# Who fills the query rows with zeros: ScalarE in eight pieces in the place of two GpSimd memsets

## The chip, the cores and the metric

The kernel runs on one core of a Trainium2 chip. Its five engines work on their own instruction streams and meet only at semaphores: TensorE (PE, with its weight loads PEld), VectorE (DVE), ScalarE (ACT), GpSimd (POOL) and SyncE (SP), which here issues the DMAs. The metric is the device time of one execution in microseconds; lower is better. Three executions of the kernel before took 801.71, 802.96 and 804.95 us, so the median is 802.96 us.

## The reference

The program computes three residual steps on x, which is 2 x 1024 tokens of width 256:

```python
x = x + 0.5 * ffn(layernorm(x))      # silu(x Wg) * (x Wu), 2 of each 4 kept by size, then Wd; inner width 1024
x = x + attention(layernorm(x))      # 32 query heads, 8 key/value heads, head size 8, rotary, causal
x = x + 0.5 * ffn(layernorm(x))      # the same weights
```

In attention, q, k and v come from one projection of the normed x, q and k are turned by the rotary tables, and each group of four query heads shares one key/value head:

```python
q = x @ Wq + bq ; k = x @ Wk + bk ; v = x @ Wv + bv
q = q*cos + rotate_half(q)*sin ; k = k*cos + rotate_half(k)*sin
attn = softmax(causal(q k^T / sqrt(8))) ; out = (attn v) @ Wo + bo
```

Two batches times eight key/value heads make 16 groups, each with 4 query heads over 1024 tokens.

## The kernel before

**Phases.** The program is four phases, one after the other on each engine: the first feed-forward network, the projection to q, k and v, attention over 16 groups, the second feed-forward network. Matmuls that must keep float32 precision are done as three products of high and low parts (hi x hi, hi x lo, lo x hi), so every operand is split: a copy rounded to the multiplier's format makes the high part, and a subtraction makes the low part.

**The projection phase** is the one that the change touches. It goes over four chunks c = 0 to 3 of 512 tokens, and in each chunk over three units u = 0, 1, 2 (two halves of q, and k). A unit passes through the engines like this:

- PE multiplies (L218, twelve matmuls of 512 columns for a unit), signals `qk_done`. Between unit 1 and unit 2 of a chunk it transposes the normed x of the next chunk (`normed.transpose`, L188), for which it waits for DVE's `v_ready` (L733) and `xn_ready`. After unit 0 it does the matmuls for v (L751).
- DVE adds the bias and multiplies by cos and by sin (L815, L817), and signals `by_ready`.
- POOL adds the two products: `qkv_turned` (L859).
- ACT copies that to the high part in `qkv_parts` (L790, `high`).
- POOL subtracts for the low part (L864, `low`).
- SP stores both parts to DRAM (L895), as rows that attention will load.

POOL takes the units strictly in order, `add_turned` then `low` then the next `add_turned`, so it waits for ACT in the middle of each unit. ACT, too, has one order, written out in `chunk`: high part of unit 0; the first half of the next chunk's transposed x (L195); high part of unit 1; the second half of the transposed x (L195 again, after all units of the chunk are multiplied); high part of unit 2. The second half of the transposed x is thus queued behind the high part of unit 1. DVE does the normalisation of the chunk after the next transposes (`normalise`, L181, four instructions of 128x256 from SBUF to SBUF), then unit 0, the values v (L823), unit 1, the statistics, the low parts of the transposed x (L199), unit 2.

**The rows of the groups.** `GroupRows` holds two sets of tiles, e = 0 and 1: `q[e]`, 128 partitions by 4 heads by 1024 tokens, and `k[e]`, 128 by 1024. Only some partitions of them are loaded; the others must hold zeros in q and -1 in k. So before the first load into set e, the whole tile is filled, once in the program: `fill_q` (L961) and `fill_k` (L964), both POOL memsets, and SP waits for them in front of `load_m` (L902, L908). They stand in the list `fills`, of which POOL does item c after chunk c (L878): q0 after chunk 0; k0 and the causal mask (L1635, L1637, in `before_groups`) after chunk 1; q1 and k1 after chunk 2.

**Into attention.** The first four products of attention (`first_scores`) stand ahead of the last unit of chunk 3 on PE. After them comes a lead-in: PE multiplies q by k for the row maxima (L1371), DVE takes the maxima (L1471, L1474), POOL splits them into shifts (L1586, L1588), PE transposes the shift (L1379), ACT copies it (L1530), SP writes it into the q rows (L1647), and only then do the scores that ACT exponentiates start (L1406, L1524), followed by the products with v (L1422).

## Time and profile before

| what | value |
|---|---|
| median of three executions | 802.96 us (801.71 to 804.95) |
| span of the profiled execution, first to last instruction | 799.2 us |
| the profiled execution's own time | not recorded apart from its span; the median is 3.8 us above that span |
| PE busy / DVE busy | 752.0 us (94%) / 712.8 us (89%) |
| ACT busy / POOL busy | 487.9 us (61%) / 263.3 us (33%) |
| mean granted PE clock | 0.974 of full speed |
| projection phase | from about 172 to 221 us of the span |
| the two q fills on POOL | 3.52 us each |
| the two k fills on POOL | 0.95 us each |

How to read it: times are from the start of the span. Busy shares over the whole span mix phases with different limits; the change lies in the 50 us of the projection phase, and what it is worth is read there. A row of a timeline gives start, duration, engine, line, operation, and in brackets how long the engine had been idle before it and which instruction released it. Back-to-back instructions of DVE, ACT and POOL are shown with a small overlap, since the next one starts before the last has fully ended.

### The profile page before, as it was taken

The page shows a single profiled execution, that of the slowest core. Times are in us where ns is not written, and L with a number is a line of the kernel's source. Part 1 is how long each engine was busy: PE and PEld are TensorE (multiplying, and loading weights), DVE is VectorE, ACT ScalarE, POOL GpSimd, SP SyncE. Part 2 cuts the span into 40 slices and gives each one's busy share as a digit, 9 for nine tenths or more (in the row PEclk, how much of TensorE's full clock was granted, in tenths as well). Part 3 has the DMA queues.
Part 4 walks back from the last instruction along what each step waited for, and adds up shares of the span by engine and source line. Part 5 has one row for each costly group of instructions (what it writes and reads, how often), then busy time and mean ns, then how long its engine had stood idle before and what let it go on. Part 6 is the DMA issues. An engine that isn't in the chain of part 4 may idle for free.

```text
span 799.2 us, 15470 instructions
## 1 busy us (share of the span) xinstructions
PE 752.0 (94%) x5168; PEld 503.9 (63%) x5168; DVE 712.8 (89%) x1857; ACT 487.9 (61%) x949; POOL 263.3 (33%) x359
## 2 busy tenths in 40 slices
PE   4899999988999999999999999999999999999996
PEld 3677887886855444554444544444544577888886
DVE  4989999988598999999999999999996459989997
ACT  6454443321124888888888888888888634344451
POOL 1143535027742222333222332255335211533330
PEclk9999999999965999999999999999999999999998
DMA  8100000015753033431133321633223000000001
GB/s 305 44 12 1 1 1 1 1 52 185 218 179 68 11 70 76 89 73 43 40 76 75 75 62 47 159 78 76 62 55 75 16 8 1 1 27 1 27 1 52
DMA packets 23551, 48.83 MB, mean 61 GB/s; under 512 B 3784, under 2 KB 10568, under 8 KB 22960
## 3 DMA queue, kind: packets, MB, share of 16 engines
q1 hardware_dynamic: 23408, 47.78, 22.8%
q8 instruction: 41, 0.67, 0.4%
q14 instruction: 38, 0.31, 0.1%
q10 hardware_dynamic: 64, 0.07, 0.0%
HBM read 19.83 MB, written 14.35 MB: 43 GB/s over the span
## 4 chain that ended last, share of the span: by engine, by line
PE 64%; DVE 19%; POOL 6%; issue 5%; ACT 4%; DMA 1%; PEldq 0%; PEld 0%; SPq 0%; DVEq 0%; ACTq 0%; POOLq 0%
PE att_o_ps L1422 18%; PE att_s_ps L1406 15%; PE att_m_ps L1371 11%; PE ffn_gate L218 6%; PE ffn_up L218 5%; PE ffn_y_ps L351 5%; DVE ffn_hs L524 3%; DVE ffn_h L566 3%; POOL qkv_turned L859 2%; POOL qkv_parts L864 2%; PE att_m_ps L1379 1%; DVE att_scratch L1471 1%; DVE ffn_rank L510 1%; DVE ffn_pair_max L498 1%; PE out_y_ps L1162 1%
## 5 line engine op out<-in xcount | busy, mean ns | idle before, releaser
L1524 ACT ACTIVATE att_probs<-att_s_ps 128x512 f32<-128x512 f32 x630 | 305.7, 555 | 54.7 <-PE att_s_ps L1406 52.9
L1471 DVE CUSTOM_DVE_ANT_0 att_scratch<-att_m_ps,att_causal 128x512 bf16<-128x512 f32 (+3 forms) x512 | 221.1, 486 | 7.7 <-PE att_m_ps L1371 6.1
L1371 PE MATMUL att_m_ps<-k,q 64*128 64x512 f32 (+3 forms) x768 | 222.8, 399 | 2.4 <-DVE att_maxima L1471 1.9
L1406 PE MATMUL att_s_ps<-q,k 64*128 64x512 f32 (+2 forms) x756 | 209.9, 384 | 2.7 <-ACT att_probs L1524 1.0
L1406 PEld LDWEIGHTS att_s_ps<-q,k 64*128 64x128 f32 x756 | 118.2, 188 | 97.0 <-ACT att_probs L1524 91.5
L1474 DVE TENSOR_REDUCE att_maxima<-att_m_ps 128x1 f32<-128x512 f32 x256 | 161.9, 684 | 7.2 <-PE att_m_ps L1371 7.1
L1422 PE MATMUL att_o_ps<-att_probs,att_vs 128*32 128x512 f32 (+3 forms) x1536 | 158.5, 500 | 3.2 <-POOL att_probs L1563 1.6
L1563 POOL TENSOR_SCALAR_AFFINE_SELECT att_probs<-att_probs 128x512 f32<-128x512 f32 x128 | 80.0, 637 | 245.3 <-ACT att_probs L1524 245.3
L1371 PEld LDWEIGHTS att_m_ps<-k,q 64*128 64x128 f32 x768 | 128.1, 193 | 42.0 <-DVE att_maxima L1471 24.4
L630 POOL TENSOR_TENSOR ffn_hs_lo<-ffn_hs,ffn_hs_hi 128x512 fp32r<-128x512 f32 x48 | 76.7, 1622 | 106.5 <-ACT ffn_hs_hi L427 106.5
L454 ACT ACTIVATE ffn_a<-ffn_h 128x512 f32<-128x512 f32 x64 | 40.5, 633 | 106.3 <-DVE ffn_h L566 106.3
L351 PE MATMUL ffn_y_ps<-wd_hi,ffn_hs_hi 128*128 128x256 f32 x256 | 73.8, 288 | 6.3 <-DVE x L554 2.7
L351 PE MATMUL ffn_y_ps<-wd_lo,ffn_hs_hi 128*128 128x256 f32 x256 | 72.9, 285 | 0.0
L351 PE MATMUL ffn_y_ps<-wd_hi,ffn_hs_lo 128*128 128x256 f32 x256 | 72.8, 284 | 0.0
L1422 PEld LDWEIGHTS att_o_ps<-att_probs,att_vs 128*32 128x32 f32 x1536 | 34.1, 108 | 54.9 <-issue 42.0
L566 DVE TENSOR_TENSOR ffn_h<-ffn_up,ffn_silu 128x512 f32<-128x512 f32 x64 | 43.6, 682 | 22.8 <-ACT ffn_silu L449 21.8
L218 PE MATMUL ffn_gate<-ffn_xt_hi,wg_hi 128*128 128x512 f32 x128 | 52.2, 408 | 4.7 <-DVE ffn_h L566 2.7
L351 PEld LDWEIGHTS ffn_y_ps<-wd_hi,ffn_hs_hi 128*128 128x128 f32 x256 | 49.4, 193 | 9.4 <-DVE x L554 2.9
L218 PE MATMUL ffn_gate<-ffn_xt_lo,wg_hi 128*128 128x512 f32 x128 | 50.8, 397 | 0.9 <-DVE ffn_xt_lo L199 0.9
L427 ACT ACTIVATE ffn_hs_hi<-ffn_hs 128x512 fp32r<-128x512 f32 x56 | 35.0, 633 | 27.1 <-DVE ffn_hs L524 27.1
L218 PE MATMUL ffn_gate<-ffn_xt_hi,wg_lo 128*128 128x512 f32 x128 | 50.9, 398 | 0.0
L351 PEld LDWEIGHTS ffn_y_ps<-wd_lo,ffn_hs_hi 128*128 128x128 f32 x256 | 49.5, 193 | 1.6
(117 smaller groups left out, 1176.5 us busy)
## 6 DMA issues: line engine op xcount, KB each, us to landing
q_rows<-qkv_parts SPq DMA_DIRECT2D x16, 512.0 KB, 4.0
q<-q_rows SPq DMA_DIRECT2D x16, 512.0 KB, 4.7
q<-q SPq DMA_DIRECT2D x16, 512.0 KB, 4.3
q<-att_shift_t SPq DMA_DIRECT2D x132, 4.0 KB
k_rows<-qkv_parts SPq DMA_DIRECT2D x8, 256.0 KB, 3.0
k<-k_rows SPq DMA_DIRECT2D x16, 128.0 KB, 4.9
k<-k SPq DMA_DIRECT2D x16, 128.0 KB, 4.6
out_num<-att_sums SPq DMA_DIRECT2D x128, 16.0 KB
```

The source lines that it names most:

```text
L218: last = pe.matmul(bank, w[w_part], xt[:, k, :], start=(k == 0 and n == 0), stop=(k == self.KT - 1 and n == 2))
L351: last = pe.matmul(y_ps[:, t, :], hp[:, blk, j, rows], wp[:, blk, j, :], start=(blk == 0 and j == 0 and m == 0 and t % 2 == 0), stop=(blk ...
L454: act.activation(a[:, blk, j, :], h[:, blk, j, :], ACT.Abs).then_inc(abs_ready, 1)
L566: dve.tensor_tensor(h[:, blk, j, :], gu[j % 2][1][:], silu[:, j % 2, :], ALU.mult).then_inc(h_ready, 1)
L630: pool.tensor_tensor(hs_lo[:, blk, j, :], hs[:, j, :], hs_hi[:, blk, j, :].bitcast(F32), ALU.subtract).then_inc(lo_ready, 1)
L1371: pe.matmul(m_ps[unit_bank(n)][:, COLUMNS[m]], q[g % 2][m_lane, h, t * P:(t + 1) * P], k[g % 2][m_lane, kc * N:kc * N + cols], start=True, ...
L1406: last = pe.matmul(s_all[S_BANK[n]][:, at:at + w], k[g % 2][lane, kb * P:(kb + 1) * P], q[g % 2][lane, h, qc * N + q0:qc * N + q0 + w], st ...
L1422: last = pe.matmul(o_ps[32 * h:32 * (h + 1), q0:q0 + w], vs[g % 2][:, kb, :], probs[u % len(probs)][:, h, at:at + w], start=(u in CHUNK_FI ...
L1471: dve.tensor_tensor_reduce(out=scratch[bank][:, at], in0=m_ps[bank][:, at], in1=causal[:, N - n:], scale=1.0, scalar=LOWEST, op0=ALU.add, ...
L1474: dve.tensor_reduce(top_of, m_ps[bank][:, at], mybir.AxisListType.X, ALU.max).then_inc(m_taken, 1)
L1524: act.activation(probs[u % len(probs)][:, h, SPAN[u]], s_all[S_BANK[n]][:, SPAN[u]], ACT.Exp, scale=SCALE).then_inc(exp_done, 1)
L1563: pool.affine_select(out=blk, in_=blk, compare_op=ALU.is_ge, fill=0.0, base=0, pattern=[[0, QPK], [1, P]], channel_multiplier=-1).then_inc ...
```

## The change

The q fills move from POOL to ACT. Each 128x4096 memset becomes four ACT copies of 128x1024, one for each head, whose input is a one-column zero tile read again and again. The zero tile is set by one small POOL memset at the start of the phase. Set 0 is filled behind the high part of unit 2 in chunk 0, set 1 behind the high part of unit 2 in chunk 1. On POOL, the k0 fill moves up into the place of the q0 fill (behind chunk 0), the causal mask stays behind chunk 1, and only the k1 fill is left behind chunk 2. SP waits for ACT's fills on a new semaphore beside the old one.

```diff
--- before.py
+++ after.py
@@ -782,6 +782,8 @@
         dve.wait_ge(w_hi_ready, 1)
         dve.tensor_tensor(w_lo[:], w_raw, w_hi[:].bitcast(F32), ALU.subtract).then_inc(w_lo_ready, 1)
 
+    FILLS = {(e, UNITS - 1): [(e, h) for h in range(group_rows.QPK)] for e in range(2)}
+
     def scalar(act):
         def high(c, u):
             n = c * UNITS + u
@@ -796,11 +798,14 @@
                     act.wait_ge(normed.xt_used, FIRST + c + 1)
                     normed.high_parts(act, FIRST + c + 1, 0)
                 high(c, u)
+                for e, h in FILLS.get((c, u), ()):
+                    group_rows.fill_q(act, e, h)
                 if turn:
                     act.wait_ge(qk_done, (c + 1) * UNITS)
                     for k in range(1, KT):
                         normed.high_parts(act, FIRST + c + 1, k)
 
+        act.wait_ge(group_rows.zero_ready, 1)
         for c in range(0, CHUNKS - 1):
             chunk(c)
         chunk(CHUNKS - 1, last=True)
@@ -871,6 +876,7 @@
                 if u == 1 and c + 2 < CHUNKS:
                     normed.inverse_deviation(pool, FIRST + c + 2)
 
+        pool.memset(group_rows.zero[:], 0.0).then_inc(group_rows.zero_ready, 1)
         normed.inverse_deviation(pool, FIRST + 1)
         for c in range(CHUNKS):
             chunk(c)
@@ -899,13 +905,15 @@
         for c in range(FIRST_BATCH):
             store(c)
         group_rows.wait_stored(sp, FIRST_BATCH)
-        sp.wait_ge(group_rows.filled, 2)
+        sp.wait_ge(group_rows.filled, 1)
+        sp.wait_ge(group_rows.q_filled, group_rows.QPK)
         group_rows.load_m(sp, 0)
         for c in range(FIRST_BATCH, CHUNKS):
             store(c)
             if c == FIRST_BATCH:
                 group_rows.copy_s(sp, 0)
-                sp.wait_ge(group_rows.filled, 4)
+                sp.wait_ge(group_rows.filled, 2)
+                sp.wait_ge(group_rows.q_filled, 2 * group_rows.QPK)
                 group_rows.load_m(sp, 1)
 
     def banks_free(pe, bank):
@@ -943,7 +951,10 @@
             self.at[e] = region.at
             self.q.append(region.take(f"q{e}", [P, self.QPK, T], F32R))
             self.k.append(region.take(f"k{e}", [P, T], F32R))
+        self.zero = region.take("zero", [P, 1], F32)
+        self.zero_ready = ctx.enter_context(nc.semaphore("zero_ready"))
         self.filled = ctx.enter_context(nc.semaphore("rows_filled"))
+        self.q_filled = ctx.enter_context(nc.semaphore("rows_q_filled"))
         self.s_loaded = [ctx.enter_context(nc.semaphore(f"s_loaded{e}")) for e in range(2)]
 
         self.m_loaded = [ctx.enter_context(nc.semaphore(f"m_loaded{e}")) for e in range(2)]
@@ -957,8 +968,8 @@
             for sem in sems:
                 sp.wait_ge(sem, 16 * chunks)
 
-    def fill_q(self, pool, e):
-        pool.memset(self.q[e][:].rearrange("p h t -> p (h t)").bitcast(F32), 0.0).then_inc(self.filled, 1)
+    def fill_q(self, act, e, h):
+        act.activation(self.q[e][:, h, :], self.zero[:].to_broadcast([P, self.T]), ACT.Copy).then_inc(self.q_filled, 1)
 
     def fill_k(self, pool, e):
         pool.memset(self.k[e][:].bitcast(F32), -1.0).then_inc(self.filled, 1)
@@ -1823,9 +1834,7 @@
         output = Output(nc, ctx, late, hole, x, w_o.rearrange("(k p) n -> p k n", p=P), den_rows, inverse_rows, KVH, C // HD // KVH, HD, T, N, out_ps)
         attention, before_groups, first_scores, first_maxima, hooks = attention_programs(
             nc, ctx, group_rows, v, att_region, s_ps, m_ps, m_spare, o_ps, output, normed2, ident_bf, x, bo, T, HD, earlier)
-        between["fills"] += [lambda pool: group_rows.fill_q(pool, 0),
-                    lambda pool: (group_rows.fill_k(pool, 0), before_groups(pool)),
-                    lambda pool: (group_rows.fill_q(pool, 1), group_rows.fill_k(pool, 1))]
+        between["fills"] += [lambda pool: group_rows.fill_k(pool, 0), before_groups, lambda pool: group_rows.fill_k(pool, 1)]
         between["first_scores"], between["first_maxima"] = first_scores, first_maxima
         assert att_region.at <= late_at
         homes2 = Homes(s_hole, {**dict.fromkeys(("ffn2_silu", "ffn2_rank", "ffn2_both_low", "ffn2_tilt"), late_hole), "ffn2_hs": m_hole})
```

On POOL, the rows around the end of chunk 0 and the end of chunk 1, before (line 859 adds the two rotary products, line 864 subtracts for the low part, k_52 and q_51 are the tiles of set 0):

```order
L859 TENSOR_TENSOR qkv_turned<-qkv_by_cos,qkv_by_sin 128x512
L864 TENSOR_TENSOR qkv_parts<-qkv_turned,qkv_parts 128x512
L961 MEMSET q_51 128x4096
L859 TENSOR_TENSOR qkv_turned<-qkv_by_cos,qkv_by_sin 128x512
...
L864 TENSOR_TENSOR qkv_parts<-qkv_turned,qkv_parts 128x512
L964 MEMSET k_52 128x1024
L1635 MEMSET att_causal 128x512
L1637 AFFINE_SELECT att_causal<-att_causal 128x128
L859 TENSOR_TENSOR qkv_turned<-qkv_by_cos,qkv_by_sin 128x512
```

The same stretch of POOL in the changed kernel, where lines 859 and 864 have become 864 and 869:

```order
L864 TENSOR_TENSOR qkv_turned<-qkv_by_cos,qkv_by_sin 128x512
L869 TENSOR_TENSOR qkv_parts<-qkv_turned,qkv_parts 128x512
L975 MEMSET k_52 128x1024
L864 TENSOR_TENSOR qkv_turned<-qkv_by_cos,qkv_by_sin 128x512
...
L869 TENSOR_TENSOR qkv_parts<-qkv_turned,qkv_parts 128x512
L1646 MEMSET att_causal 128x512
L1648 AFFINE_SELECT att_causal<-att_causal 128x128
L864 TENSOR_TENSOR qkv_turned<-qkv_by_cos,qkv_by_sin 128x512
```

Behind chunk 0 a memset of 4096 columns has given way to one of 1024, and behind chunk 1 the k fill is gone from ahead of the mask.

On ACT, from the last unit of chunk 0 to the first unit of chunk 2, before (line 790 is the high part of a unit, line 195 a half of the transposed x):

```order
L195 ACTIVATE ffn_xt_hi<-ffn_xt_ps 128x512
L790 ACTIVATE qkv_parts<-qkv_turned 128x512 x2
L195 ACTIVATE ffn_xt_hi<-ffn_xt_ps 128x512
L790 ACTIVATE qkv_parts<-qkv_turned 128x512
L195 ACTIVATE ffn_xt_hi<-ffn_xt_ps 128x512
L790 ACTIVATE qkv_parts<-qkv_turned 128x512 x2
```

The same stretch of ACT in the changed kernel, with the high part now at line 792:

```order
L195 ACTIVATE ffn_xt_hi<-ffn_xt_ps 128x512
L792 ACTIVATE qkv_parts<-qkv_turned 128x512
L972 ACTIVATE q_51<-zero 128x1024 x4
L792 ACTIVATE qkv_parts<-qkv_turned 128x512
L195 ACTIVATE ffn_xt_hi<-ffn_xt_ps 128x512
L792 ACTIVATE qkv_parts<-qkv_turned 128x512
L195 ACTIVATE ffn_xt_hi<-ffn_xt_ps 128x512
L792 ACTIVATE qkv_parts<-qkv_turned 128x512
L972 ACTIVATE q_53<-zero 128x1024 x4
L792 ACTIVATE qkv_parts<-qkv_turned 128x512
```

Each pair of high parts that ran over the end of a chunk now has four fill copies between its two members. PE's and DVE's own order is unchanged.

## Rows read from the trace of the kernel before

**Rows 1.** The page: engines, and the chain that ended last by engine.
```profile
PE 752.0 (94%) x5168; PEld 503.9 (63%) x5168; DVE 712.8 (89%) x1857; ACT 487.9 (61%) x949; POOL 263.3 (33%) x359
...
PE 64%; DVE 19%; POOL 6%; issue 5%; ACT 4%; DMA 1%; PEldq 0%; PEld 0%; SPq 0%; DVEq 0%; ACTq 0%; POOLq 0%
```
**Rows 2.** Timeline of PE: start us, us, instruction, [idle before, releaser].
```profile
174.60 1.09 PE L188 MATMUL ffn_xt_ps<-ident,ffn_xn 128*128 128x128 f32 x8 [1.88 <-DVE v L823]
...
190.85 1.94 PE L188 MATMUL ffn_xt_ps<-ident,ffn_xn 128*128 128x128 f32 x8 [3.65 <-DVE qkv_by_sin L817]
...
204.38 1.03 PE L188 MATMUL ffn_xt_ps<-ident,ffn_xn 128*128 128x128 f32 x8
...
209.98 0.50 PE L218 MATMUL qkv_plain<-ffn_xt_hi,qkv_w_hi 128*128 128x512 f32 x1 [0.38 <-ACT ffn_xt_hi L195]
...
231.12 0.59 PE L1379 MATMUL att_m_ps<-ident_bf,att_shift 128*8 128x128 bf16 x4 [0.26 <-POOL att_shift L1588]
```
**Rows 3.** Timeline of DVE around the normalisation behind chunk 0.
```profile
182.26 6.84 DVE L181 TENSOR_SCALAR ffn_xn<-x,ffn_mean_var,ffn_rstd 128x256 f32<-128x256 f32 x4 [0.20 <-POOL ffn_rstd L175]
189.02 0.73 DVE L815 SCALAR_TENSOR_TENSOR qkv_by_cos<-qkv_plain,qkv_biases,qkv_cos 128x512 f32<-128x512 f32 x1
...
190.34 0.41 DVE L823 TENSOR_TENSOR v<-ffn_xt_ps,qkv_bv 128x256 f32<-128x256 f32 x1
```
**Rows 4.** Line 181 alone, 186 to 190 us and whole span: min/median/max ns.
```profile
L181 DVE TENSOR_SCALAR ffn_xn<-x,ffn_mean_var,ffn_rstd x1: 4922/4922/4922, 184.2 to 184.2; 128x256 f32<-128x256 f32 x1
...
L181 DVE TENSOR_SCALAR ffn_xn<-x,ffn_mean_var,ffn_rstd x48: 400/406/4922, 10.4 to 733.9; 128x256 f32<-128x256 f32 x48
```
**Rows 5.** Timeline of POOL, projection phase.
```profile
184.21 1.29 POOL L864 TENSOR_TENSOR qkv_parts<-qkv_turned,qkv_parts 128x512 fp32r<-128x512 f32 x1 [0.74 <-ACT qkv_parts L790]
185.44 3.52 POOL L961 MEMSET q<- 128x4096 f32 x1
190.50 1.27 POOL L859 TENSOR_TENSOR qkv_turned<-qkv_by_cos,qkv_by_sin 128x512 f32<-128x512 f32 x1 [1.54 <-DVE qkv_by_sin L817]
...
199.02 1.37 POOL L859 TENSOR_TENSOR qkv_turned<-qkv_by_cos,qkv_by_sin 128x512 f32<-128x512 f32 x1 [0.31 <-DVE qkv_by_sin L817]
...
202.36 0.95 POOL L964 MEMSET k<- 128x1024 f32 x1
203.25 0.53 POOL L1635 MEMSET att_causal<- 128x512 f32 x1
...
204.20 1.29 POOL L859 TENSOR_TENSOR qkv_turned<-qkv_by_cos,qkv_by_sin 128x512 f32<-128x512 f32 x1
...
215.29 3.52 POOL L961 MEMSET q<- 128x4096 f32 x1
```
**Rows 6.** Timeline of ACT, chunks 1 and 2.
```profile
191.80 0.63 ACT L790 ACTIVATE qkv_parts<-qkv_turned 128x512 fp32r<-128x512 f32 x1 [7.67 <-POOL qkv_turned L859]
...
208.81 0.63 ACT L790 ACTIVATE qkv_parts<-qkv_turned 128x512 fp32r<-128x512 f32 x1 [1.37 <-POOL qkv_turned L859]
209.35 0.58 ACT L195 ACTIVATE ffn_xt_hi<-ffn_xt_ps 128x512 fp32r<-128x512 f32 x1
```
**Rows 7.** ACT groups by form, 238 to 247 us: count, busy us, mean ns.
```profile
L1524 ACT ACTIVATE att_probs<-att_s_ps 128x512 f32<-128x512 f32 x8 | 4.3, 597 | 0.4 <-PE att_s_ps L1406 0.2
L1524 ACT ACTIVATE att_probs<-att_s_ps 128x256 f32<-128x256 f32 x4 | 1.4, 383 | 1.0 <-PE att_s_ps L1406 1.0
```
**Rows 8.** Windows: PE, PEld, DVE, ACT, POOL busy, then granted clock.
```profile
190.80:194.20 3.40, 3.35 (x12) 3.09 (x13) 2.90 (x10) 0.63 (x1) 2.66 (x3) 0.51 0.26 98
225.00:249.00 24.00, 23.39 (x72) 14.23 (x72) 23.59 (x84) 8.84 (x16) 8.66 (x18) 0.50 0.31 98
249.00:259.00 10.00, 10.00 (x45) 4.70 (x49) 7.19 (x24) 3.50 (x7) 0.61 (x3) 0.50 0.62 136
259.00:279.00 20.00, 19.55 (x170) 9.49 (x162) 18.99 (x70) 16.86 (x37) 4.59 (x10) 1.00 0.03 6
```
**Rows 9.** Timeline of SP's queue: the first load of set 0.
```profile
205.60 0.34 SPq L975 DMA_DIRECT2D q<-q_rows  x1
```

## The prediction, made before the changed kernel was run

> **What bounds the kernel now.** Read the page first [rows 1]: PE is busy 94% of the span and holds 64% of the chain that ended last, while the engine that loses work here, POOL, is busy 33%. Taken over the span, 7 us of POOL time would be worth nothing. So look at the one place where the chain runs through POOL, the projection phase, and ask PE's timeline where PE stood still [rows 2]. The reader is to see one large hole: before the transposes behind unit 1 of chunk 1 PE is idle 3.65 us, up to 190.85. It waits for DVE. DVE's timeline [rows 3] shows why DVE is late: four normalisations took 6.84 us together, and the values v, on which the transposes also wait, came only at 190.34. The rows of line 181 alone [rows 4] show that one of the four, started at 184.2, took 4.92 us, where the median of all 48 is 0.41 us. POOL's timeline [rows 5] has the cause: the low part ran from 184.21 to 185.50 and the q0 memset from 185.44 to 188.96, and the slow instruction ended at 189.10, 0.14 us behind the memset. The same POOL waited 1.54 us afterwards, for the DVE that it had held up.
>
> The second thing to see is what carries a delay on. At 209.98 PE waits again, 0.38 us, for the second half of the transposed x on ACT [rows 2]. That copy stands at 209.35 right behind the high part of unit 1, which had waited for POOL's `qkv_turned` [rows 6]. So from chunk 2 on the tight chain is POOL to ACT to PE, and PE's own earliness counts only as far as that chain follows.
>
> Attention then takes the shift over whole. From 259 us PE is busy 19.55 of 20 us at full clock, and in the lead-in from 225 to 249 us DVE is busy 23.59 of 24 [rows 8]. Work that is full on one engine starts earlier and ends earlier, and nothing in it is tied to a time.
>
> **The change, part by part.**
>
> *q0 memset away, k0 memset in its place.* What stands behind the low part of chunk 0 falls from 3.52 to 0.95 us [rows 5]. I take it that the blocked normalisation waits through this memset as it did through the longer one, and so ends at 186.5, not 189.1: 2.57 us earlier. Bounds: none of it, if something else had held that instruction (0), and all of the memset (3.5) if the k fill is not waited for. I choose 2.57, since the end of the slow instruction sits 0.14 us behind the end of the memset, and a k fill is the same instruction with fewer columns.
>
> The Trainium skill speaks against this reading of the blocking. "SBUF — State Buffer", section "Who interferes with whom", says that DVE in a two-port mode and GpSimd exclude each other for the whole of one instruction, and that issue order decides who blocks. By that the waiting DVE instruction would have got in at 185.5, between the low part and the memset; the trace shows it waiting through both. Page and row agree that the two block each other, but not on when the loser gets its turn. I go by the row; the other reading is a rival below, 0.7 us better.
>
> *The clock.* In the stretch 190.8 to 194.2 the granted clock is 0.51, the lower level of 1.2 GHz, behind the idle 3.65 us, and the eight transposes take 1.94 us against 1.03 in the next chunk [rows 2, 8]. At half speed 3.35 us busy hold 1.7 us of full-speed work, so the low stretch costs 1.7. With the hole cut to 3.65 - 2.57 = 1.1 us I expect no fall: the idle 1.88 us before 174.60 brought none, as the transposes after it took 1.09 us [rows 2]. PE is then 2.6 + 1.7 = 4.3 us earlier. Bounds 0 and 1.7.
>
> *What the POOL chain lets through.* POOL starts chunk 1 2.57 us earlier, at 187.9. Walking its three units with the durations of the rows (1.29 for each sum and difference, 0.74 for the trip to ACT and back), the sum of unit 2 comes at 195.7 instead of 199.02 [rows 5]: 3.3 us, since PE's halves of x are no longer late as well. Then the k0 fill is gone from between chunks 1 and 2, 0.9 us with its overlap, and the first sum of chunk 2 starts at 200.0 instead of 204.20: 4.2 us.
>
> *The new ACT copies.* A copy of 128x1024 is not in the trace. The exponentials of 512 and 256 columns take 597 and 383 ns, so 256 columns cost 214 and 1024 columns about 1.03 us, four of them 4.1, or 3.9 when they overlap [rows 7]. Bounds: 0.60 each, as for 512 columns, and 1.19, two of 512, so 2.4 to 4.8 us for four. Behind chunk 0 they run from 184.15 to about 188.1, and the next high part is wanted at 189.2; before, ACT sat idle 7.67 us here [rows 6], so they are free even at the upper bound. What stands behind them is only that high part. Behind chunk 1 there is less room: the high part of unit 2 would end near 197.8, the copies near 201.8, and POOL's first sum of chunk 2 is ready at 201.3. The high part waits 0.5 us, and POOL, DVE and PE behind it. Bounds 0 and 1.3. So 4.2 - 0.5 = 3.7 us arrive where PE waits at 209.98, less than PE's own 4.3.
>
> *Chunk 2's fills.* The q1 memset, 3.52 us at 215.29 [rows 5], is not on PE's path: the sums behind it feed stores and nothing that PE reads. It does hold back the first shift of attention: PE waited 0.26 us for it at 231.12 [rows 2]. That wait goes, and what is late next is DVE's maxima, 3.7 us earlier like the rest. I count 0.2.
>
> *Waits and queues.* SP now waits for the q fill (done by 188.2) and the k fill (186.4) before its load of set 0, which went out at 205.60 behind the stores of chunk 1 [rows 9]. These stores end last by 13 us or more, so the new wait is free; its cover is chunk 1's own stores. For set 1 the fills end near 201.8 on ACT and 212 on POOL, long before the lead-in needs that set. The zero tile's memset runs where POOL waits for DVE, and the first ACT wait on it follows that by microseconds: 0.
>
> Sum against the profiled execution: 3.7 + 0.2 = 3.9 us off a span of 799.2, giving 795.3. The median stands 3.8 above that span, so the time is 802.96 - 3.9 = 799.1 us.
>
> **The rivals.**
>
> *Only the stall goes (2.6 us).* The clock falls at 187 all the same, or the four copies cost their upper bound behind chunk 1, so that 3.7 shrinks to 2.9 or less. For it: in the lead-in the clock is low from 225 us on although PE counts as busy 23.39 of 24 us [rows 8], so a long hole is not the only thing that brings it down. Against it: the 1.88 us before 174.60. Time 802.96 - 2.6 = 800.4.
>
> *The waiting instruction gets in at once.* If DVE's fourth normalisation runs between low part and k fill, it ends 0.7 us sooner, and the chain is 0.7 us further ahead: 4.6 us, 798.3. The 4.92 us of [rows 4] speak against it. (It is what the rule of the Trainium skill in "SBUF — State Buffer" would give.)
>
> *The low clock in the lead-in ends sooner.* From 225 to 259 the clock is at its low level [rows 8]. To 249 that costs next to nothing, as DVE is full. From 249 to 259 DVE is busy only 7.19 of 10 us, against 18.99 of 20 afterwards, so these 10 us cost 2.3. A lead-in shifted by 4 us might meet the rise earlier: up to 2.3 more, 796.8.
>
> *The stall was hidden anyway.* Another wait takes the place of the hole, for instance ACT's halves of x held by POOL in chunk 1 as in chunk 2. The walk above leaves them 3.3 us or more ahead, which speaks against it. Time 803.0.
>
> *Slower: the low clock lasts into attention's steady part.* It rose at 259, when products with v had begun to fill PE. There PE has no slack (19.55 of 20 us), and each further low microsecond costs between 0.24, as from 249 to 259, and 0.5, half the speed. If the shifted lead-in misses the rise by 15 us, it costs 7.5: 802.96 - 3.9 + 7.5 = 806.6. It decides from 3.9 / 0.5 = 8 us on. Against it: the instruction order on PE is the same, and the rise comes with that order.
>
> **How the numbers follow.** Within 0.5% (4.0 us) a measurement of this kernel can't tell from no change, and the forecast of 3.9 lies on that edge. Chances: forecast 0.46, only the stall 0.20, in at once 0.05, low clock sooner 0.13, hidden 0.08, slower 0.08. The forecast splits about evenly over the edge, so faster is 0.23 + 0.05 + 0.13 + a little from a base that shifts = 0.44, same 0.23 + 0.20 + 0.06 = 0.49, slower 0.07. The range: the forecast's own is 797.8 to 800.4; it must reach 796.8 less a little for the noise of 1.6 us half-width, and up to the hidden case: 795.8 to 802.8. Outside are the slower case, half of the hidden one, and the tail below.
>
> **What would show it right or wrong.** In the profile after: line 181 in chunk 0 with a slowest instruction near 2.35 us (4.92 less 2.57); PE's wait before the second set of transposes near 1.1 us, and their eight matmuls in 1.0 to 1.1 us at clock 1.00; POOL's first sum of chunk 2 at 200 to 200.5 us; four ACT copies in 3.9 to 4.1 us; ACT's high part of unit 0 in chunk 2 right behind the fourth copy, without a wait for POOL; the first load of set 0 some 3 us earlier, released by the stores. The forecast is wrong if the slow normalisation stays at 4.9 us, if PE's hole moves instead of shrinking, or if the windows at full clock begin later than 259 us.

## The result, and the profile after

The changed kernel took 797.57 us in the median (797.05 to 800.30, 6 runs) against 802.44 us of the kernel before (6 runs, the three from above among them). One of the six runs before, 830.46 us, was slow as a whole and is left out of the ratio, so the ratio is not the quotient of these two medians (0.9939). It is 0.9951, 95% interval [0.9934, 0.9967]: 0.49% faster, or 3.9 us of the 802.96 that the forecast started from, with 2.6 to 5.3 us inside the interval. The forecast was 799.1, that is 0.9952. The profiled span fell from 799.2 to 796.1 us.

The profile's page shows what moved: POOL lost 6.7 us of busy time, ACT gained 7.3, and POOL's share of the chain halved from the 6% of [rows 1].

```profile
PE 752.0 (94%) x5168; PEld 504.4 (63%) x5168; DVE 709.1 (89%) x1857; ACT 495.2 (62%) x957; POOL 256.6 (32%) x358
...
PE 66%; DVE 19%; issue 5%; ACT 5%; POOL 3%; DMA 1%; PEldq 0%; PEld 0%; SPq 0%; DVEq 0%; ACTq 0%; POOLq 0%
```

PE's timeline after, for [rows 2] (L1390 is the old L1379):

```profile
174.52 1.40 PE L188 MATMUL ffn_xt_ps<-ident,ffn_xn 128*128 128x128 f32 x8 [1.93 <-DVE v L828]
...
188.19 1.04 PE L188 MATMUL ffn_xt_ps<-ident,ffn_xn 128*128 128x128 f32 x8
...
200.77 1.06 PE L188 MATMUL ffn_xt_ps<-ident,ffn_xn 128*128 128x128 f32 x8 [0.47 <-DVE qkv_by_sin L822]
...
227.21 0.59 PE L1390 MATMUL att_m_ps<-ident_bf,att_shift 128*8 128x128 bf16 x4
```

The hole of 3.65 us is gone altogether, not cut to 1.1, and so is the wait for `ffn_xt_hi` at 209.98. A wait of 0.47 us stands before the third transposes. I measure every kernel below from the first row to the last of these, from chunk 0's transposes to the first transposes of attention's shift; call it the **stretch**. It was 231.12 - 174.60 = 56.52 us before and is 52.69 after: 3.83 less.

DVE's normalisations after, behind chunks 0 and 1, for [rows 3], and line 181 over the whole span, for [rows 4]:

```profile
182.67 2.33 DVE L181 TENSOR_SCALAR ffn_xn<-x,ffn_mean_var,ffn_rstd 128x256 f32<-128x256 f32 x4
...
195.18 3.85 DVE L181 TENSOR_SCALAR ffn_xn<-x,ffn_mean_var,ffn_rstd 128x256 f32<-128x256 f32 x4 [0.19 <-POOL ffn_rstd L175]
```

```profile
L181 DVE TENSOR_SCALAR ffn_xn<-x,ffn_mean_var,ffn_rstd x48: 396/408/1933, 10.2 to 730.8; 128x256 f32<-128x256 f32 x48
```

Behind chunk 0 four normalisations took 2.33 us together: the slowest took 1.36 us, through one POOL instruction (the sum at 182.83), and none waited through the k fill. The slowest of all 48, 1.93 us, is now behind chunk 1. It started at 197.1 and so waited through the low part and the mask's memset, to 199.03.

POOL's timeline after, for [rows 5]:

```profile
184.94 1.29 POOL L869 TENSOR_TENSOR qkv_parts<-qkv_turned,qkv_parts 128x512 fp32r<-128x512 f32 x1 [0.74 <-ACT qkv_parts L792]
186.16 0.95 POOL L975 MEMSET k<- 128x1024 f32 x1
187.08 1.29 POOL L864 TENSOR_TENSOR qkv_turned<-qkv_by_cos,qkv_by_sin 128x512 f32<-128x512 f32 x1
189.24 1.30 POOL L869 TENSOR_TENSOR qkv_parts<-qkv_turned,qkv_parts 128x512 fp32r<-128x512 f32 x1 [0.87 <-ACT qkv_parts L792]
...
195.11 1.26 POOL L864 TENSOR_TENSOR qkv_turned<-qkv_by_cos,qkv_by_sin 128x512 f32<-128x512 f32 x1
197.12 1.29 POOL L869 TENSOR_TENSOR qkv_parts<-qkv_turned,qkv_parts 128x512 fp32r<-128x512 f32 x1 [0.74 <-ACT qkv_parts L792]
198.35 0.53 POOL L1646 MEMSET att_causal<- 128x512 f32 x1
...
200.42 1.28 POOL L864 TENSOR_TENSOR qkv_turned<-qkv_by_cos,qkv_by_sin 128x512 f32<-128x512 f32 x1 [1.09 <-DVE qkv_by_sin L822]
```

The 1.09 us in the last row is the new wait: POOL, freed of the k fill here, waits for the DVE that it has blocked. ACT's timeline after, for [rows 6]:

```profile
184.76 3.88 ACT L972 ACTIVATE q<-zero 128x1024 fp32r<-128x1024 f32 x4
188.55 0.61 ACT L792 ACTIVATE qkv_parts<-qkv_turned 128x512 fp32r<-128x512 f32 x1
...
196.95 3.88 ACT L972 ACTIVATE q<-zero 128x1024 fp32r<-128x1024 f32 x4
201.73 0.63 ACT L792 ACTIVATE qkv_parts<-qkv_turned 128x512 fp32r<-128x512 f32 x1 [0.91 <-POOL qkv_turned L864]
```

Four copies take 3.88 us. Behind chunk 0 the high part follows them at once, and POOL waits 0.87 us for it instead of the usual 0.74: there the copies fill ACT's gap and 0.13 us more. Behind chunk 1 ACT is done 0.91 us before it is wanted, so these copies are hidden. The windows after, for [rows 8]:

```profile
225.00:249.00 24.00, 23.70 (x79) 14.14 (x78) 22.13 (x81) 8.21 (x15) 4.12 (x10) 0.50 0.16 44
249.00:257.00 8.00, 8.00 (x46) 3.92 (x46) 5.78 (x16) 4.20 (x8) 0.00 (x0) 0.50 0.60 138
257.00:277.00 20.00, 19.54 (x162) 9.69 (x160) 19.06 (x69) 16.97 (x36) 4.57 (x10) 1.00 0.04 10
```

The clock is back at its upper level, 2.4 GHz, from 257 us on, 2 us earlier than before, although the work came 3.8 us earlier.

### The profile page after: what moved, and what is told of

Its sections match the earlier page's. It is cut to its first block, busy times and chain, and to the rows that moved or that the text cites. A ratio compares the mean times of both kernels' runs of the same rounds, so it can differ in the third digit from the quotient of the medians.

```text
span 796.1 us, 15479 instructions
## 1 busy us (share of the span) xinstructions
PE 752.0 (94%) x5168; PEld 504.4 (63%) x5168; DVE 709.1 (89%) x1857; ACT 495.2 (62%) x957; POOL 256.6 (32%) x358
## 4 chain that ended last, share of the span: by engine, by line
PE 66%; DVE 19%; issue 5%; ACT 5%; POOL 3%; DMA 1%; PEldq 0%; PEld 0%; SPq 0%; DVEq 0%; ACTq 0%; POOLq 0%
PE att_o_ps L1433 18%; PE att_s_ps L1417 15%; PE att_m_ps L1382 12%; PE ffn_gate L218 5%; PE ffn_up L218 5%; PE ffn_y_ps L351 5%; DVE ffn_h L566 3%; DVE ffn_hs L524 3%; DVE att_scratch L1482 2%; PE att_m_ps L1390 1%; DVE ffn_rank L510 1%; DVE ffn_pair_max L498 1%; DVE ffn_pair_min L499 1%; PE out_y_ps L1173 1%; DVE ffn_first_wins L501 1%
## 5 line engine op out<-in xcount | busy, mean ns | idle before, releaser
L566 DVE TENSOR_TENSOR ffn_h<-ffn_up,ffn_silu 128x512 f32<-128x512 f32 x64 | 43.6, 681 | 22.9 <-ACT ffn_silu L449 21.9
L218 PE MATMUL ffn_up<-ffn_xt_hi,wu_hi 128*128 128x512 f32 x128 | 50.4, 394 | 0.0
```

The lines of the kernel that those rows point to most:

```text
L218: last = pe.matmul(bank, w[w_part], xt[:, k, :], start=(k == 0 and n == 0), stop=(k == self.KT - 1 and n == 2))
L566: dve.tensor_tensor(h[:, blk, j, :], gu[j % 2][1][:], silu[:, j % 2, :], ALU.mult).then_inc(h_ready, 1)
```

## The experiments

Two theories compete; each expectation spells out its own. **P**: the chain POOL to ACT to PE of the projection pays for every microsecond that POOL spends on fills behind chunks 0 and 1, and the 3.65 us hole was only the face of it that showed. **L**: the price is the lock, the normalisation held by POOL, with PE's hole and the fallen clock. All ratios are to the kernel before, for e1 to e12 run on the same chip as the experiment, with 95% intervals; each stretch is from one trace; the stretch was 56.52 us before.

| run | ratio | stretch, us |
|---|---|---|
| the change | 0.9951 [0.9934, 0.9967] | 52.69 |
| the change again (e9) | 0.9952 [0.9935, 0.9969] | 52.64 |
| q0 alone on ACT (e1) | 0.9968 [0.9953, 0.9983] | 53.43 |
| the same again (e10) | 0.9956 [0.9942, 0.9969] | 53.05 |
| q1 alone on ACT (e2) | 0.9998 [0.9985, 1.0010] | 55.34 |
| before, memset in four (e3) | 1.0011 [1.0000, 1.0023] | 56.23 |
| before, q0 and k0 fills swapped (e4) | 1.0020 [1.0005, 1.0035] | 57.02 |
| all eight copies behind chunk 0 (e5) | 0.9993 [0.9980, 1.0006] | 55.66 |
| before, ACT normalises (e6) | 1.0011 [0.9995, 1.0027] | 59.67 |
| the change, ACT normalises (e7) | 0.9962 [0.9948, 0.9975] | 53.82 |
| the change, k0 fill behind chunk 1 (e8) | 0.9959 [0.9943, 0.9975] | 53.54 |
| half of the q0 fill on ACT (e11) | 0.9971 [0.9959, 0.9982] | 54.54 |
| the change, mask late (e12) | 0.9952 [0.9933, 0.9971] | 52.91 |

**One part alone: e1 and e2.**

```diff
-    FILLS = {(e, UNITS - 1): [(e, h) for h in range(group_rows.QPK)] for e in range(2)}
+    FILLS = {(e, UNITS - 1): [(e, h) for h in range(group_rows.QPK)] for e in (0,)}   # e1; (1,) in e2
```

The other set keeps its memset on POOL, at its old place (in e2 the k0 fill, too).

> Only the q0 fill moves to ACT (and the k0 fill into its place behind chunk 0); the q1 fill stays a 3.52 us POOL memset behind chunk 2. Theory: the whole gain comes from what POOL no longer does behind chunk 0, and the fill behind chunk 2 is off PE's path but for the first shift (0.2 us). So ratio about 0.9953 to the kernel before (797.57/802.44 is 0.994 to 0.9967 by the runs), and POOL's first sum of chunk 3 near 216 instead of 212.41 us with no later PE. Rival: the q1 fill is worth as much as the q0 fill, since both are 3.52 us of POOL: then the ratio is about 0.998.

> Only the q1 fill moves to ACT, behind chunk 1; the q0 memset stays behind chunk 0 and the k0 fill behind chunk 1, as before. Theory: PE's hole of 3.65 us and the low clock after it stay, so the ratio is 1.000 (0.9990 to 1.0005); ACT's four copies behind chunk 1 are hidden. Rival: each fill is worth half, ratio 0.998; second rival, the copies are in the way, ratio 1.001.

The q0 fill carries the gain: 0.9968 for it alone (e10 measures it again, at 0.9956), and no difference that can be measured for q1 alone. The telling thing is PE's timeline of e2, where the q0 memset is still on POOL:

```profile
186.69 1.06 PE L188 MATMUL ffn_xt_ps<-ident,ffn_xn 128*128 128x128 f32 x8 [0.19 <-issue]
190.95 0.47 PE L218 MATMUL qkv_plain<-ffn_xt_hi,qkv_w_hi 128*128 128x512 f32 x1 [0.39 <-ACT ffn_xt_hi L195]
194.12 0.50 PE L218 MATMUL qkv_plain<-ffn_xt_hi,qkv_w_hi 128*128 128x512 f32 x1 [1.54 <-ACT ffn_xt_hi L195]
202.78 1.06 PE L188 MATMUL ffn_xt_ps<-ident,ffn_xn 128*128 128x128 f32 x8 [1.52 <-DVE qkv_by_sin L822]
```

Here the hole before the second transposes is missing, the clock did not fall, and yet the time is that of before (0.9998; the interval allows 1.2 us less). The normalisations behind chunk 0 took 3.38 us: the last one got in ahead of the memset. PE instead stood three times, 3.45 us in all, for ACT's halves of x behind POOL's late sums and for DVE behind chunk 1. That speaks for P, but it is no kernel without a lock: behind chunk 1 the normalisations were blocked for 4.75 us in all. Nor is the long lock free. Up to here e2 and before are the same program but for the zero tile's small memset, and POOL's first sum of chunk 1 comes 14.50 us behind the transposes of chunk 0 in e2, against 15.90 before. Of these 1.40 us 1.03 are left at the first sum of chunk 2, behind the second lock.

**Memset in four pieces, and swapped with the k fill: e3 and e4** (both on the kernel before).

```diff
+        for h in range(self.QPK):                                             # e3
+            last = pool.memset(self.q[e][:, h, :].bitcast(F32), 0.0)
-        between["fills"] += [lambda pool: group_rows.fill_q(pool, 0),         # e4
-                    lambda pool: (group_rows.fill_k(pool, 0), before_groups(pool)),
+        between["fills"] += [lambda pool: group_rows.fill_k(pool, 0),
+                    lambda pool: (group_rows.fill_q(pool, 0), before_groups(pool)),
```

> The kernel before with each q memset split in four POOL memsets of 1024 columns (0.95 us each, so 3.6 to 3.8 us for four), nothing on ACT. Theory A, the blocked DVE instruction waits until POOL pauses, however many instructions follow each other: line 181's longest in chunk 0 stays near 4.9 to 5.2 us and the ratio is 1.000. Theory B, it gets in at the end of the one POOL instruction that blocks it: line 181's longest is 1.3 to 1.7 us, the hole of PE is under 1 us, and the ratio is 0.995 to 0.997.

> The kernel before with the fills of set 0 exchanged, all on POOL: k0 behind chunk 0, q0 with the causal mask behind chunk 1. Theory: behind chunk 0 it looks like the changed kernel (no hole of 3.65 us), but POOL's first sum of chunk 2 comes 3.5 us later than in the changed kernel (near 204) and PE meets it at chunk 3: about 3 of the 4.9 us are given back, ratio 0.9975 to 0.999. Rival: only what stands behind chunk 0 matters, ratio 0.9950.

In e3 the four pieces took 3.63 us together, and the normalisations behind chunk 0 did not meet them (2.33 us), as DVE had got ahead of POOL. So it says nothing on borders between the pieces. It speaks for P like e2: behind chunk 0 no long lock and no hole, and the time of before. It too has a lock behind chunk 1, 4.74 us for the four, with PE idle for 1.50 us. In e4 I expected a gain and was wrong. The memset met the normalisations behind chunk 1 in full:

```profile
194.78 7.29 DVE L181 TENSOR_SCALAR ffn_xn<-x,ffn_mean_var,ffn_rstd 128x256 f32<-128x256 f32 x4 [0.18 <-POOL ffn_rstd L175]
```

```profile
203.82 1.69 PE L188 MATMUL ffn_xt_ps<-ident,ffn_xn 128*128 128x128 f32 x8 [4.06 <-DVE qkv_by_sin L817]
```

The loss is not tied to chunk 0. Moved by one chunk, it comes back whole.

**How much ACT hides: e5**, all eight copies behind chunk 0.

```diff
+    FILLS = {(0, UNITS - 1): [(e, h) for e in range(2) for h in range(group_rows.QPK)]}
```

> The changed kernel, but all eight ACT copies stand behind chunk 0 (none behind chunk 1). They take 7.8 us there instead of 3.9, from about 184.8 to 192.5, and the high part of unit 0 of chunk 1 is wanted at about 188.4. Theory: ACT's cover behind chunk 0 ends after some 3.6 us, so about 4 us are lost on the chain from POOL over ACT to PE and the gain is gone: ratio 0.999 to 1.001 to the kernel before. Rival: ACT has room, since it is busy only 62% of the span: ratio 0.995 as in the changed kernel.

```profile
188.15 1.28 POOL L864 TENSOR_TENSOR qkv_turned<-qkv_by_cos,qkv_by_sin 128x512 f32<-128x512 f32 x1 [1.54 <-DVE qkv_by_sin L822]
192.51 1.29 POOL L869 TENSOR_TENSOR qkv_parts<-qkv_turned,qkv_parts 128x512 fp32r<-128x512 f32 x1 [3.08 <-ACT qkv_parts L792]
```

Eight copies took 7.66 us and held the high part that POOL waits for: 3.08 us against the usual 0.74. ACT's gap behind a chunk takes the four copies of the change and no more, and the gain is gone (0.9993).

**The lock taken out: e6 and e7.** ACT makes the normalised x of chunks 2 and 3, from x times 1/deviation and a shifted mean that POOL works out, so that DVE has no normalisation there that POOL could block; e6 is the kernel before with this, e7 the changed one.

```diff
+            act.activation(self.xn[:, t, :], self.x_tile(c, t), ACT.Identity, bias=self.minus_mean[:, t:t + 1],
+                           scale=self.rstd[:, t:t + 1]).then_inc(self.xn_ready, 1)
-        if c + 1 < CHUNKS:
+        if c == 0:
             normed.normalise(dve, FIRST + c + 1)
```

> The kernel before, all fills on POOL, but the normalised x of chunks 2 and 3 is made by ACT (with two small POOL instructions for its bias), so no instruction of DVE in these chunks can be blocked by POOL. Theory L, the loss is DVE standing blocked behind the memset: without the block the gain is there although the memset stays, ratio 0.995 to 0.997. Theory P, the loss is the 3.5 us that the memset keeps POOL from its next sum, whoever is blocked: ratio 0.999 to 1.001, PE waits about 1.5 us for ACT's half of x in chunk 2 as in the run with only q1 moved.

> The changed kernel with the normalised x of chunks 2 and 3 made by ACT in the same way. Theory P: the block behind chunk 1 (3.85 us for four instructions, POOL waiting 1.09 us for DVE and PE 0.47 us) goes, against about 0.5 us of added POOL work in each of two chunks and 1.3 us of added ACT work: ratio 0.994 to 0.9955, at best 0.5 us better than the changed kernel. Theory L: another 1.5 us, ratio 0.993.

POOL and PE in e6:

```profile
186.68 3.52 POOL L981 MEMSET q<- 128x4096 f32 x1
190.16 1.26 POOL L878 TENSOR_TENSOR qkv_turned<-qkv_by_cos,qkv_by_sin 128x512 f32<-128x512 f32 x1
```

```profile
192.72 0.47 PE L233 MATMUL qkv_plain<-ffn_xt_hi,qkv_w_hi 128*128 128x512 f32 x1 [1.99 <-ACT ffn_xt_hi L210]
195.88 0.80 PE L233 MATMUL qkv_plain<-ffn_xt_hi,qkv_w_hi 128*128 128x512 f32 x1 [1.07 <-ACT ffn_xt_hi L210]
```

Without any lock in these chunks the kernel before is not faster (1.0011), and the change on top of it still gains: e7 stands at 0.9962. L had the first at 0.995 to 0.997. The aid has a price of its own, and e7 is slower than the 0.994 to 0.9955 that I gave it: ACT's four normalisations take 2.08 us ahead of a high part, for which POOL then waits 1.5 us. So only the difference of e6 and e7 speaks on the memset, 0.5% in time and 5.85 us in the stretch.

Part of that difference is the clock. Behind the wait of 1.99 us PE's clock fell in e6 and stayed low from 193.6 to 207.1 us, while in e7 it was 1.00 from 193 to 207. One window of PE in e6 (busy, then clock):

```profile
196.00:198.00 2.00, 2.00 (x5) 0.50 0.94 337
```

The clean comparison is the one ahead of that fall. POOL's first sum of chunk 1 comes 15.70 us behind the transposes in e6 and 13.20 in e7: 2.50 less, where the two fills on POOL differ by 3.52 - 0.95 = 2.57, with full clock and with no normalisation on DVE. At the first sum of chunk 2 it is 3.17 less; the rest of the 5.85 arises behind it.

**The k0 fill back behind chunk 1: e8** (on the changed kernel).

```diff
-        between["fills"] += [lambda pool: group_rows.fill_k(pool, 0), before_groups, ...
+        between["fills"] += [lambda pool: None, lambda pool: (group_rows.fill_k(pool, 0), before_groups(pool)), ...
```

> The changed kernel, but the k0 fill stays behind chunk 1 with the mask, as before the change, so nothing stands behind chunk 0 on POOL. Theory P: 0.95 us of POOL has only moved from one chunk to the next, ratio 0.9945 to 0.996, no difference to the changed kernel that can be measured. Rival, from my prediction: the k fill gone from chunk 1 was worth 0.9 us, so this kernel is 0.9 us slower than the changed one, ratio 0.9962.

The stretch is 0.85 us longer, about the 0.95 of the fill; the ratios 0.9959 and 0.9951 can't be told apart. So in the stretch the rival, the term of my prediction, was right, and a fill is not worth the same wherever it stands. Behind chunk 0 taking it away gave nothing, as POOL then waited for ACT's copies:

```profile
189.15 1.29 POOL L869 TENSOR_TENSOR qkv_parts<-qkv_turned,qkv_parts 128x512 fp32r<-128x512 f32 x1 [1.55 <-ACT qkv_parts L792]
```

That is 14.65 us behind the transposes, against 14.72 with the k0 fill there (the change). P holds for what POOL spends beyond ACT's copies.

**The change and e1 again: e9 and e10**, word for word the same programs.

> The changed kernel once more, beside the next three on one chip. Theory P (3.5 us of GpSimd time taken out of the chain of the projection phase): ratio 0.995 to 0.996 again, from the transposes of chunk 0 to attention's first transposes 52.7 us as in the first profile. If the hundredths that decide who gets in between two GpSimd instructions vary from run to run of one program, the normalisation behind chunk 0 may now be the blocked one (one instruction of 2.3 us) and that behind chunk 1 not; by P the 52.7 us stay within 0.4.

> The q0 fill alone on ScalarE, the q1 fill left as a memset, measured against the whole change on one chip. The earlier profiles give the q1 fill 0.7 us (53.4 us against 52.7 from the transposes of chunk 0 to attention's first transposes), so ratio 0.0009 above the whole change. If the q1 fill is worth nothing, both ratios agree within 0.0005.

e9 repeats the change: 0.9952, 52.64 us, and again 2.33 us of normalisation behind chunk 0. e10 did not repeat e1's trace: 4.28 us there in e1, 2.33 here, with a stretch of 53.43 and 53.05. Their stretches are 0.4 us apart, and their ratios 0.0004, which is nothing that can be measured. But that 0.4 is not the q1 fill: 0.32 of it is there at POOL's low part of unit 2 in chunk 0, ahead of every fill. From POOL's first sum of chunk 2 to the end of the stretch it takes 26.79 us in e9 and 26.88 in e10, and so it is in all traces without ACT's normalisation: 26.77 to 26.80 where the q1 fill is on ACT, 26.87 to 27.00 where it is on POOL. The q1 fill is worth 0.1 us there; e4 alone stands apart, with the fills exchanged.

**Half the dose: e11**, two heads on ACT, two in a POOL memset ahead of the k0 fill.

```diff
+        pool.memset(self.q[e][:, 2:4, :].rearrange("p h t -> p (h t)").bitcast(F32), 0.0).then_inc(self.filled, 1)
```

> Of the q0 fill two heads go to ScalarE and two stay on GpSimd, one memset of 128x2048, 1.8 us by half of 3.52, ahead of the k0 fill; everything else as in the changed kernel. Theory P, the price is proportional to GpSimd's time: 1.8 us later than the changed kernel at attention's first transposes, 54.5 us instead of 52.7, ratio 0.9973. Rival, the price comes only from the long lock with its idle TensorE and fallen clock: with a blocked normalisation of at most 4.1 us and no fall of the clock most of the gain stays, 53 us, ratio 0.9955.

```profile
185.79 1.81 POOL L975 MEMSET q<- 128x2048 f32 x1
187.54 0.95 POOL L978 MEMSET k<- 128x1024 f32 x1
188.45 1.30 POOL L864 TENSOR_TENSOR qkv_turned<-qkv_by_cos,qkv_by_sin 128x512 f32<-128x512 f32 x1
```

```profile
194.24 0.50 PE L218 MATMUL qkv_plain<-ffn_xt_hi,qkv_w_hi 128*128 128x512 f32 x1 [1.20 <-ACT ffn_xt_hi L195]
202.00 1.06 PE L188 MATMUL ffn_xt_ps<-ident,ffn_xn 128*128 128x128 f32 x8 [0.60 <-DVE qkv_by_sin L822]
```

1.81 us of POOL cost 1.85 to 1.90 us of stretch against the two traces of the change, and 1.49 against e10, with no normalisation behind chunk 0 that waits through a fill (2.33 us) and no hole there. The 0.3 us that these traces differ by ahead of any fill bound how well that is known. P named 54.5 us and 0.9973; measured are 54.54 and 0.9971. L's 53 us is out. Its 0.9955 lies just outside the interval, which begins at 0.9959; as e1 and e10, one program, differ by 0.0012, the ratio alone would not decide it.

**The mask away from behind chunk 1: e12.**

```diff
+        between["fills"] += [lambda pool: group_rows.fill_k(pool, 0), lambda pool: None, lambda pool: (before_groups(pool), group_rows.fill_k(pool, 1))]
```

> The changed kernel with the causal mask's memset and select (0.53 and 0.30 us) moved from behind chunk 1 to behind chunk 2, ahead of the k1 fill. In the changed kernel they stand between the chunks, the normalisation behind chunk 1 waits through them (1.93 us), and TensorE waits 0.47 us. Theory P: the first sum of chunk 2 comes 0.6 to 1.0 us earlier (199.5 to 199.8 instead of 200.4), and attention's first transposes 0.5 to 1 us earlier if the same two instructions behind chunk 2 feed nothing TensorE waits for; ratio 0.994 to 0.995. If the steps behind chunk 1 are not on the chain any more: no difference from the changed kernel.

No difference from e9 (0.9952 both); the gain I gave it did not come. The normalisations behind chunk 1 did shrink, from 3.85 to 3.39 us, but behind chunk 0 they took 4.28 us in this trace, and POOL stood 1.54 us for DVE at both places. POOL's third sum of chunk 1 came 0.73 us later in the stretch than in e9, its first of chunk 2 only 0.27 us later: the mask's share is the 0.46 us between. No version beat the change.

## Why the prediction was right

The forecast of 3.9 us less came out: 3.83 and 3.88 us of stretch in two traces, ratios 0.9951 and 0.9952. The mechanism held in its core: the fill on POOL held back the chain POOL to ACT to PE. Several terms were wrong in size, and they cancelled. That the sum came out to a tenth of a microsecond is luck, as the interval of the ratio alone reaches from 2.6 to 5.3 us.

*The blocked normalisation waits through the k fill: 2.57 us.* In the change's two traces it did not: DVE was through at 185.0, when the low part had only just begun. From PE's first transposes to POOL's first sum of chunk 1 it is 15.90 us before and 12.56 after, 3.34 less, not 2.57. But where the lock did occur, the step was right to the hundredth: in e12 line 181 alone reads, behind chunk 0,

```profile
L181 DVE TENSOR_SCALAR ffn_xn<-x,ffn_mean_var,ffn_rstd x4: 399/878/2358, 181.6 to 183.5; 128x256 f32<-128x256 f32 x4
```

against my "near 2.35 us", PE's wait was 1.07 us, and e1's first sum of chunk 1 came 13.38 us behind the transposes, 2.52 less than before. Both alignments belong to one program (e1 and e10).

*The clock: 1.7 us.* The low stretch of [rows 8] at 190.8 is gone, and the second transposes took 1.04 us. But I argued that an idle 1.88 us brings no fall of the clock. Behind the 1.93 us in the trace after it fell. Windows of PE (busy, then clock), of the changed kernel and of e12:

```profile
174.00:179.00 5.00, 4.48 (x17) 0.66 0.39 142
```

```profile
174.00:179.00 5.00, 4.90 (x25) 1.00 0.52 193
```

So the ground was false, though the conclusion for the later place stood. Behind a wait of 1.9 us the clock may fall or not.

*The chain's walk: 3.3 at the third sum of chunk 1, 4.2 at the first sum of chunk 2, less 0.5 for the copies.* Measured within the stretch: 3.83, then 3.70. The third sum was further ahead than I said, and between the two sums nothing was gained on balance. The k0 fill that is gone there was worth its 0.85 us, as e8 shows, but POOL now waited 1.09 us for DVE, which it had blocked with the low part and the mask; before it had not waited there. I had looked for the late thing on ACT (0.5 us, in truth 0 with 0.91 us to spare) and it was on DVE. Behind chunk 0, where I had called the copies free even at their upper bound, they made POOL wait 0.13 us more. 3.7 was predicted and 3.70 measured, by other terms.

*Copies, q1, queues.* Four copies 3.9 to 4.1 us: 3.88. The q1 fill 0.2: 0.1 by the rows behind the first sum of chunk 2; PE's wait for the shift, 0.24 us in e10, is gone. The first load of set 0, 3 us earlier and released by the stores: 201.63 against 205.60 [rows 9], 4.0 earlier; no new wait of SP showed.

*The reading of the bottleneck.* I called the hole the thing to remove, and the POOL chain what limits how much of it counts. The runs put the larger part on the chain. POOL's fill is paid for without a lock (e6 and e7: 2.50 us for 2.57 at the first sum of chunk 1), without the long lock behind chunk 0 (e2, e3), at another chunk (e4), and at half size (e11). The long lock adds its own part, which I first took for the whole: e2, which does the same work up to there without it, is 1.40 us ahead at the first sum of chunk 1, and 1.2 us in the stretch, though its time is no better. From e2 to the change it is another 2.65 us, and that is the q0 fill gone and the k0 fill put in its place. So of the 3.83 us some 2.7 are POOL's time and some 1.1 the lock and the q1 fill, an estimate from single traces. The forecast survived since the walk along POOL gave the smaller number and I took that.

*The rivals.* "Only the stall goes" (800.4 / 802.96 = 0.9968) lies at the edge of both intervals of the change (upper ends 0.9967 and 0.9969); the stretch, 3.8 us and not 2.6 shorter in both traces, speaks against it. "Hidden anyway" is out. "Low clock of the lead-in ends sooner" did not happen after: the rise came 29.8 us behind the stretch's end against 27.9 before, and from there to the end of the span it took 568.9 us against 568.1. In e1, e8, e11 and e12 the rise came 21.5 to 21.9 us behind it, and the rest took 567.8, 568.7, 568.8 and 567.5 us; in the others 567.1 to 570.9. That is why the span shrank by 3.1 us and the stretch by 3.83. What an early rise is worth isn't settled by single traces. The slower rival did not occur.

## What to carry to other kernels

Work on a lightly used engine costs up to its full time where that engine is a link of a chain, and nothing where the chain waits for another engine at that place (the k0 fill behind chunk 0); judge it by the chain's walk from one fixed instruction to another, not by the largest idle gap, which may be just one of the forms that the same delay takes. Before you take a gap for the price, look whether another kernel or trace of the same length has the gap elsewhere. Moving work pays if the new host has a gap of that length at that place, four copies and not eight here, and the engine that comes next has to be sought among all that feed the chain.

## What the runs showed of the hardware

**Between two POOL instructions the waiting DVE instruction mostly loses.** In the twelve traces in which DVE normalises behind chunks 0 and 1, a normalisation was waiting at twenty borders between one POOL instruction and the next. At eighteen it did not get in: it waited through the low part and what stood behind it, the q0 memset (before, 4.92 us), the k fill (e1, e5, e12, 2.36 us) or the mask's memset (the change among others, 1.93 us), and in e2, e3 and e8 through three, low part, k fill and mask (2.83 us), in e4 through low part, q0 memset and mask (5.37 us). It got in where POOL stopped, if only for the 0.15 us between the mask's memset and the select. At the other two, in e2 and e4 behind chunk 0, it got in between low part and memset, and the memset was the longer one:

```profile
184.73 3.67 POOL L974 MEMSET q<- 128x4096 f32 x1
```

```profile
185.23 1.11 POOL L964 MEMSET k<- 128x1024 f32 x1
```

Those are 0.15 us more than the 3.52 and 0.95 of [rows 5]. The rule of the Trainium skill ("SBUF — State Buffer", section "Who interferes with whom"), exclusion for one whole instruction and the first to issue blocks the other, agrees with the waits through one POOL instruction (1.36 us in the change behind chunk 0); what the traces add is that the loser can lose again at the border, and did at eighteen of twenty. I had read getting in as a rival, at 0.05 and priced at 0.7 us; e2, the one trace where it happened with the q0 memset, is 1.40 us ahead at the first sum of chunk 1.

**A lower clock went with a shorter path.** Behind PE's wait of 1.9 us in chunk 0 the clock fell to its lower level, 1.2 GHz, for some 3.5 us in six traces (the change, e3, e8 to e11) and not in six others (before, e1, e2, e4, e5, e12). In all six of the first kind the four normalisations behind chunk 0 took 2.33 us, and in all six of the second 3.38 to 6.84. In the first kind POOL's low part of unit 2 came 10.3 to 10.7 us behind the transposes, in the second 9.6 to 9.7, and the slowest normalisation then waited through one POOL instruction (1.36 us), where in four of the second kind it waited through two. That fits a slower PE that delays ACT's halves of x, so that DVE and POOL come to the third unit in another order. The link between the two is read from twelve traces and was not forced by a run of its own. It costs or gives some tenths of a microsecond (e1 and e10: 0.4). A fall can last much longer: in e6, behind a wait of 1.99 us, 13.5 us.
